# Heads-last pieces in DRAM, eight transfers a stack, and another order at a step's end, in a kernel of four layers

## What is computed

```python
x = x + sliding_window_attention(layernorm(x))   # 32 heads of 8, window 128, blocks of 128 tokens
x = x + ffn(layernorm(x))                        # 256 -> 1024 -> 256, relu, 4-bit weights + rank 16
x = x + delta_layer(layernorm(x))                # see below
x = x + ffn(layernorm(x))                        # same weights as the second
```

```python
h = rms(x); q, k, v = silu(silu(conv4(h @ Wqkv)))    # causal convolution over 4 tokens
q, k = l2norm(q), l2norm(k);  beta = sigmoid(h @ Wbeta)
for each token:  err = S @ k - v;  S = S - beta * outer(err, k);  o = S @ q    # S: 8 x 8 per head
x = x + rms(o) @ Wout;  x = x + (silu(h2 @ Wgate) * (h2 @ Wup)) @ Wdown        # h2 = rms(x)
```

## Time and profile before

| | us |
|---|---|
| median of 3 runs (1444.98 to 1447.88) | 1446.38 |
| the profiled execution | 1451.55 |
| its span in the profile | 1449.8 |
| PE busy | 1098.5 (76%) |
| DVE busy | 938.5 (65%) |
| ACT busy | 509.6 (35%) |
| POOL busy | 174.2 (12%) |

### The profile page before, as it was taken

How to read it: one execution, slowest core, us unless ns; L and a number is a source line. 1 busy time by engine, 2 the same in 40 slices (tenths; PEclk the granted TensorE clock), 3 DMA queues, 4 the chain that set the end, 5 groups by cost and what they waited for, 6 DMA issues and landing times.

```text
span 1449.8 us, 22244 instructions
## 1 busy us (share of the span) xinstructions
PE 1098.5 (76%) x8593; PEld 738.9 (51%) x8600; DVE 938.5 (65%) x2409; ACT 509.6 (35%) x1041; POOL 174.2 (12%) x251
## 2 busy tenths in 40 slices
PE   5478778676778897879779896879778887980587
PEld 3144534453446654656446653656456644750465
DVE  2712368686877577765777577765776688768701
ACT  1033254226323543236323542335322633350121
POOL 2000000301030002100040002100040004011300
PEclk9578879879979998899878998899889998995689
DMA  9524224401530134102520135003410220020000
GB/s 292 75 19 61 22 66 53 39 30 59 61 30 23 30 73 54 9 30 73 59 25 22 36 76 48 7 30 77 63 18 22 67 18 1 15 66 0 14 8 8
DMA packets 112489, 64.57 MB, mean 45 GB/s; under 512 B 49472, under 2 KB 106752, under 8 KB 112384
## 3 DMA queue, kind: packets, MB, share of 16 engines
q1 hardware_dynamic: 106256, 57.61, 23.2%
q10 hardware_dynamic: 6128, 5.54, 1.5%
HBM read 45.55 MB, written 17.17 MB: 43 GB/s over the span
## 4 chain that ended last, share of the span: by engine, by line
PE 49%; DVE 23%; DMA 9%; ACT 8%; SPq 5%; issue 3%; ACTq 2%; POOL 1%; DVEq 0%; POOLq 0%
PE bank L1410 7%; PE bank L1660 6%; PE bank L1402 6%; PE bank L1587 4%; DMA q_stack<-m_rows 4%; PE bank L1679 4%; PE bank L1515 4%; DVE lane_buf L1144 3%; PE bank L1466 3%; DVE state L1163 3%; DVE state L1156 3%; DMA k_stack<-k_pieces 3%; DVE u_l L1151 3%; DVE mx L965 2%; PE bank L1495 2%
## 5 line engine op out<-in xcount | busy, mean ns | idle before, releaser
L680 ACT ACTIVATE probs<-bank 128x512 f32<-128x512 f32 x256 | 151.1, 597 | 276.6 <-PE bank L1500 271.6
L1515 PE MATMUL bank<-probs,v_ext 128*9 128x128 f32 x2048 | 169.8, 288 | 24.9 <-ACT probs L680 23.2
L965 DVE TENSOR_REDUCE mx<-bank 128x2 f32<-128x320 f32 x256 | 120.8, 485 | 103.5 <-PE bank L1466 99.4
L1660 PE MATMUL bank<-feat_c,wgu 128*128 128x256 f32 (+1 forms) x384 | 108.0, 441 | 53.0 <-DVE hid_c L1211 45.7
L1495 PE MATMUL bank<-tri_mask,identb 128*128 128x512 bf16 x256 | 106.9, 417 | 43.6 <-DMA q_stack<-m_rows 43.6
L1461 PE MATMUL bank<-edge_mask,identb 128*128 128x64 bf16 x512 | 64.0, 211 | 91.3 <-DVE mx L965 54.3
L334 POOL TENSOR_TENSOR lane_buf<-state,q_l 128x128 f32<-128x128 f32 x128 | 83.7, 682 | 334.6 <-DVEq L1169 334.6
L1515 PEld LDWEIGHTS bank<-probs,v_ext 128*9 128x9 f32 x2048 | 85.7, 93 | 71.1 <-issue 24.1
L1660 PEld LDWEIGHTS bank<-feat_c,wgu 128*128 128x128 f32 (+1 forms) x384 | 81.0, 216 | 76.8 <-DVE hid_c L1211 47.6
L1144 DVE TENSOR_TENSOR lane_buf<-state,til 128x128 f32<-128x128 f32 x256 | 102.4, 400 | 17.7 <-POOL lane_buf L567 10.1
L1461 PEld LDWEIGHTS bank<-edge_mask,identb 128*128 128x128 bf16 x512 | 33.9, 103 | 145.3 <-DVE mx L965 69.5
(11 more groups left out here) (160 smaller groups left out, 1785.1 us busy)
## 6 DMA issues: line engine op xcount, KB each, us to landing
k_stack<-k_pieces SPq DMA_DIRECT2D x192, 64.0 KB
q_stack<-q_pieces SPq DMA_DIRECT2D x192, 32.0 KB
k_l<-lane_k SPq DMA_DIRECT2D x8, 512.0 KB, 3.7
q_l<-lane_q SPq DMA_DIRECT2D x8, 512.0 KB, 4.7
q_pieces<-conv SPq DMA_DIRECT2D x24, 128.0 KB, 2.1
k_pieces<-conv SPq DMA_DIRECT2D x48, 64.0 KB, 2.0
tok<-in_x SPq DMA_DIRECT2D x8, 256.0 KB, 2.8
x_in<-in_x SPq DMA_DIRECT2D x8, 256.0 KB, 2.8
```

The lines of the kernel that those rows point to most:

```text
L680: act.activation(probs[:, u % 2], score_bank[u % 2][:], ACT.Exp, scale=float(DK) ** -0.5).then_inc(exp_done, 1)
L965: dve.tensor_reduce(mx[:, g, 2 * v:2 * v + 2], bank[1 + u % 2][:, 0:2 * SPAN].rearrange("p (h k) -> p h k", h=2), AX.X, ALU.max).then_inc( ...
L1515: last = pe.matmul(bank[5][row:row + VE, col:col + W], v_ext[:, b, kb, h, :], probs[:, u % 2, (hp * 2 + kb) * W:(hp * 2 + kb + 1) * W], st ...
L1660: last = pe.matmul(late_bank[i % 2][0:m, g * BT:(g + 1) * BT], wgu[:, k, g * INTER + 128 * i:g * INTER + 128 * i + m], fc[:, k], start=(k ...
```

## The change

- **Pieces in DRAM.** q's and k's columns are computed with the head as the last index (two ACT copies at the start permute `wqkv_a`, from a staging area `qk_staged`), so a row of a stack (one of the head's 8 numbers, all 16 heads of a half) is one run in DRAM: 4 KB for q, 8 KB for k, whose two blocks lie side by side and are therefore stored twice (`late`). A load has 8 DMAs in place of 13: zero rows, three of q with 16 rows, two of k with 16 rows, two of k with 8. A store has 9 DMAs as before, all of 256 B runs, but each k piece goes out twice. The pad is stored by 3 DMAs in place of 6.
- **Maxima rows.** One DMA on SP (`load_max`), behind the stack loads in SP's program, in place of three on ACT.
- **Order at a step's end.** `mlp_down` behind the delta projections and output sums; the output product and sums of squares behind it; the last FFN's up product in one piece of 8, its down product in one piece behind `pairs`. `late_tile` keeps the second half of both hidden tiles in a part of `lane_buf`; so POOL's `values_til` waits for the down product.
- **Pairs and substitution** of block n stand at the end of the body in which its projections are, not at the start of the next one, ahead of `result` on DVE. The layer norm of block n+2's input is there too. The scan is taken to begin at u = 5, and `PASS1`, `NEXT_AT` and the other tables are moved.
- `terms_of`: on DVE one instruction of 512 elements for four of 128. On ACT the scaling of y (`y_scale`) comes before the third norm's, inside attention.

```diff
-BEGIN = 8
-PASS1 = {14: (0, 0, 1), 15: (0, 2, 3), 16: (0, 4, 5), 17: (0, 6, 7)}
-PASS1.update({25 + v: (1, v) for v in range(8)})
+BEGIN = 5
+PASS1 = {13: (0, 0, 1), 14: (0, 2, 3), 15: (0, 4, 5), 16: (0, 6, 7)}
+PASS1.update({20 + v: (1, v) for v in range(8)})
-NEXT_AT = {"rstd": 3, "turn": 6, "queries": 8, "keys": 9, "second": 11, "third": 13}
-PAIRS_AT = 4
-TURN_AT = 20
+NEXT_AT = {"turn": 1, "queries": 3, "keys": 4, "second": 6, "third": 8}
+TURN_AT = 19
+TURN_NEXT_AT = 30
...
+Q_PIECES = [(0, 2 * DK, (0, 0)), (2 * DK, 2 * DK, (1, 1)), (4 * DK, 2 * DK, (0, 2))]
+K_PIECES = [(0, 2 * DK, (0, 1)), (2 * DK, 2 * DK, (0, 1)), (4 * DK, DK, (2,)), (5 * DK, DK, (0,))]
-        q_pieces = nc.dram_tensor("q_pieces", (NB, 3, HH, 128, B, W), BF16, kind="Internal").ap()
-        k_pieces = nc.dram_tensor("k_pieces", (3, HH, 128, B, W + T), BF16, kind="Internal").ap()
+        q_pieces = nc.dram_tensor("q_pieces", (NB, 3, HH, B, 128, W), BF16, kind="Internal").ap()
+        k_pieces = nc.dram_tensor("k_pieces", (NB + 1, 3, HH, B, 128, 2, W), BF16, kind="Internal").ap()
...
             def load_stacks(n, g):
...
-                for at, (i, j) in enumerate(PIECE_PAIRS):
-                    rows = slice(at * DK, (at + 1) * DK)
-                    sp.dma_start(q_stack[rows, r], q_pieces[n:n + 1, i, hh, :, b, :].rearrange(
-                        "n (h d) t -> d (n h) t", d=DK)).then_inc(stacks_in[r], 16)
-                    sp.dma_start(k_stack[rows, r], k_pieces[j, hh, :, b, n * W:n * W + 2 * W].rearrange(
-                        "(h d) t -> d h t", d=DK)).then_inc(stacks_in[r], 16)
+                qs = q_pieces[n, :, hh, b].rearrange("p (d h) t -> p d (h t)", d=DK)
+                ks = k_pieces[n, :, hh, b].rearrange("p (d h) k t -> p d (h k t)", d=DK)
+                for into, of, pairs in ((q_stack, qs, Q_PIECES), (k_stack, ks, K_PIECES)):
+                    for row, rows, ps in pairs:
+                        if len(ps) == 1:
+                            src = of[ps[0]]
+                        elif ps[0] == ps[1]:
+                            src = of[ps[0]:ps[0] + 1].broadcast_to([2, DK, of.shape[2]])
+                        else:
+                            src = of[ps[0]:ps[1] + 1:ps[1] - ps[0]]
+                        sp.dma_start(into[row:row + rows, r].rearrange("p h t -> p (h t)"), src
+                                     ).then_inc(stacks_in[r], 16)
...
             def pieces_to_dram(n):
...
-                    for hh in range(HH):
-                        sp.dma_start(k_pieces[p, hh, :, :, n * W + W:n * W + 2 * W],
+                    for late in range(2):
+                        sp.dma_start(k_pieces[n + late, p, :, :, :, 1 - late].rearrange("h b p t -> p (h b) t"),
...
+            def load_max(n, g):
+                sp.wait_ge(m_copied, n * NG + g + 1)
+                sp.dma_start(q_stack[MROW:MROW + 3, slot(n, g)], m_rows[:, g % 2, :]).then_inc(m_in[slot(n, g)], 16)
...
+                if following:
+                    load_max(n, 3)
+                if front:
                     next_stacks(n + 1, 1)
+                    load_max(n + 1, 0)
                     next_stacks(n + 1, 2)
+                    load_max(n + 1, 1)
...
+                if n >= 2:
+                    pool.wait_ge(ffn_c_done, n - 1)
                 pool.tensor_copy(first[:, :, :, :, DK], til[:, :, :, DK:KV].rearrange("p c i v -> p c v i")
...
             def max_rows(n, g):
...
-                for j in range(3):
-                    act.dma_start(q_stack[MROW + j:MROW + j + 1, slot(n, g)], m_rows[j * HPH:(j + 1) * HPH, g % 2, :]
-                                  ).then_inc(m_in[slot(n, g)], 16)
...
+            for k in range(KT):
+                last = act.copy(wqkv_a[:, k, 0:2 * D].rearrange("p (a d h) -> p a d h", d=DK, h=HPH),
+                                qk_staged[:, k].rearrange("p (a h d) -> p a d h", d=DK, h=HPH))
...
             def terms_of(engine, cs, steps=range(C)):
...
-                for v in range(VR):
-                    engine.tensor_tensor(out_terms[:, v, :, i, 0:DK], state[:, cs, v, :, C], qc[:, i, cs, :], ALU.mult)
+                if engine is nc.vector:
+                    engine.tensor_tensor(out_terms[:, :, :, i, 0:DK],
+                                         state[:, cs, :, :, C].rearrange("p c v k -> p v c k"),
+                                         qc[:, i:i + 1, cs, :].broadcast_to([128, VR, n_c, DK]), ALU.mult)
...
+                if following:
+                    til_first(n)
+                if n + 2 < NB:
+                    norm_next_apply(n + 2)
+                if following:
+                    pair_scale(n)
+                    for j in range(C - 1):
+                        til_column(n, j)
                 if tail:
                     result(s)
...
             def body(t, scan=True, tail=True, following=True, front=True):   # TensorE
...
-                if tail:
-                    mlp_down(s)
                 if following:
                     turn_a(n, 3)
-                    beta_in(n, front)
+                    beta_in(n, tail, front)
                     delta_in(n, front)
                     if scan:
                         output_sums(t, front)
                 if tail:
+                    mlp_down(s)
+                if following:
+                    if scan:
+                        output_product(t)
+                    square_sums(n)
+                if tail:
...
                     turn_c(s, 2)
-                    ffn_c_up(s, 0, HALF, following)
...
+                    ffn_c_up(s, 0, FT, following)
+                if following:
+                    pairs(n)
                 if tail:
-                    ffn_c_down(s, 0)
-                    ffn_c_up(s, HALF + 2, FT, following)
-                    ffn_c_down(s, 1)
+                    ffn_c_down(s)
```

More of the change, by code:

```diff
@@ L497, in _ @@
             load_x(1)
+            for g in range(DONE_EARLY):
+                load_max(0, g)
             body(-1, scan=False, tail=False)
@@ L815, in body @@
                 if following:
-                    attention(n, scan, front)
-                elif scan:
-                    pairs_out(t)
+                    attention(n, scan, tail, front)
                 if tail:
-                    y_scale(s)
+                    if not following:
+                        y_scale(s)
+                    turn_c(s, 1)
                 if following:
@@ L1125, in between @@
                     dn, g, step = PIECES_AT[at]
-                    before = max_piece(n + dn, g, step, before)
+                    if front or not dn:
+                        before = max_piece(n + dn, g, step, before)
                 if at in MAX_AT:
@@ L1692, in body @@
                     attention(n, scan, front)
-                elif scan:
-                    pairs(t)
                 if tail:
```

188 lines of the change are left out of this document (87 added, 101 removed).

## The result

The changed kernel takes 1496.6 us (median of 4 runs, 1493.18 to 1498.99) against 1445.74 of the kernel before (4 runs): ratio 1.0331, 95% interval 1.0295 to 1.0366. It is slower by 3.3%. The profiled execution takes 1495.14 us, its span is 1493.3.

A forecast was written before the change was run, and what follows sets the result against it. No engine is full; PE leads, with stack loads' duration on its path. Terms -4.5 - 0.4 - 3.8 - 5.0 - 0.2 - 2 = -15.9 take the profiled 1451.55 to 1435.7, median 1430.5 us; range 1370 to 1462.

The forecast's parts named there:

- rival B: Stack loads stay slow: above 11.3 us a load the saving is used up, at 12.2 us the time is 1458; chance 0.23.
- The length of a load (10.2 us): Stack load, about 12.2 us before: 8 issues take 2.8 us, the 7.4 to 7.6 behind the last stay.
- The rule quoted from the Trainium skill: Engines per transfer: largest number up to 16 dividing both patterns' slowest dimension; two for pair transfers, so 11.8 us a load.
- What a us of load costs (14 us): Each us of stack load adds one to each of two PE waits in each of seven attentions.
- Attention without the load's length: A step's attention: pairs and the 6.6 us maxima wait go, load waits of 3.2 and 4.4 come; -2.0 us.
- The end of a step (+4.2): From F, the MLP's down product before, delta projections after, to V, the next block's first values: 4.2 us longer than 42.45.
- tok_c (-3.2): PE's wait for the turned tok_c: y_scale moves ahead, so 3.2 of 3.6 us a step go.
- The first two blocks (-0.4, -3.8): First block: waits +1.4, ACT's issues -1.8, so -0.4 us; second: attention -2.0, issues -1.8, so -3.8.
- The start (-4.5): Start to the first block's values: no maxima issues on ACT, earlier third load, values at 77 for 81.46 us.
- The tail (-2 for the merged terms): Kernel's end: 16 output-term instructions a block become 4, on the path only where nothing follows; -2 us, bounds 0 and -5.
- Rival A: Stack loads become fast, 6 us or less, both waits gone, -53 us, to about 1377; chance 0.33.

The follow-up runs named there:

- e2: The changed kernel with 12 loads of 8 rows and one of zero rows in place of its 8 transfers a load: 1446.35 us, ratio to before 0.9989.
- e1: The changed kernel with pieces side by side in DRAM and pairs reordered, so each transfer reads contiguous rows: 1357.87 us, ratio to before 0.9381.
- e10: e1 with 16 unused PE products in the wait for feat_c ahead of the last FFN's up product: 1359.76 us, ratio to before 0.9365.
- e4: The kernel before with only the change's DRAM layout and 8 transfers a load, order, tables and maxima as before: 1446.94 us, ratio 0.9994.
- e7: e1 with the output terms on DVE again as four instructions of 128 elements: 1357.88 us, ratio to before 0.9365.

## Why the prediction was wrong

It said 1430.5 and is 66 us off, on the other side of no change. The direction of rival B was right, and its point, 11.3 us a load, was passed: a load takes 13.2. The 66 us divide so: at e2's load of 10.75 my own price gives 1438, 8 us more; e2 took 1446, another 8 for the terms that aren't loads; and from e2 to the changed kernel, which differ in the load's transfers alone, are 50.

- **The length of a load (10.2 us) failed.** The step was: the issues shrink from 13 to 8, "and the 7.4 to 7.6 behind the last stay". Neither held. The 8 issues take 4.4 us and not 2.8, and 8.8 us pass behind the last. What stays behind the last issue isn't a property of the destination alone. With two engines the drain is set by 448 KB at 25 GB/s for each, 9.0 us. The rule quoted from the Trainium skill ("DMA: Bandwidth & Descriptors", how many engines k) described it: this trace shows 0.12, e2 0.56, e1 0.93. By the rule the estimate was 11.8, and I gave it the smaller chance because the row of 8 destination rows looked nearer. e2 shows what my 10.2 stood for, loads with 8 rows: 10.75. The prediction lets the rule agree with the 0.68 of before; by the rule its transfers of 8 rows use 8 engines, a share of 0.50, so that the agreement was loose.
- **What a us of load costs (14 us) was too little.** Between e2 and the changed kernel lie 2.4 us of load (10.75 to 13.2) and 50 us of time, some 20 for each. The waits lie where I put them, and each us counts twice a step; in addition the granted clock is down behind each wait (after the one of 6.94 us the first values take 1.04 us for 0.62), and the start, with three loads in a row, is 6.7 us later than in e2.
- **Attention without the load's length** was right in kind: pairs gone, maxima wait gone, waits of 3.2 and 4.4 forecast and 3.32 and 4.20 in e2. In the changed kernel the part is +1.6 in place of -2.0, with waits of 5.75 and 6.94. The sum had a slip too: V+21.4 and the terms behind it give 67.2 and not 68.0, so -2.9, 4 us in five steps and in the wrong direction.
- **The end of a step (+4.2) was mis-sized**: +7.9. The chain was the right one (F is 1159.53; lanes at F+26.9 in place of 25.3, `til_first` at F+35.6 in place of 34.7), but the columns wait for the pairs, which stand behind an up product of 10.2 us that I reckoned at 7.0, at the clock of before. e10 shows that the idle ahead of it is the cause. One us more was lost before that, with the delta projections at 0.63: the copy to feat_c, forecast at F+27.1, ends at F+28.2. The term is +7.2 in e1 too, so it has nothing to do with loads.
- **tok_c (-3.2)**: the wait fell by 2.9, from 3.6 to 0.7; the stretch it lies in gained only 0.9, as PE's work in it takes 10.0 us and not 8.0, at a granted clock of 0.63.
- **The first two blocks (-0.4, -3.8)** were +15.9 and +5.1. The first is 123.0 in e4, with the same transfers and the old order, and 123.8 in e1, with fast loads and the new order, so order and slow loads do it together. One wait is new, and no term of mine had it: PE stands 8.7 us for the products ahead of the pairs in each of the two blocks without a tail, and the next scores are queued behind. It is there in e1 too.
- **The start (-4.5)** was +4.2: V of block 0 at 85.6, in e1 at 71.8.
- **The tail (-2 for the merged terms)**: last V to the end fell by 8.5, and in e7 no part of it comes from merging. The scan starts right behind V there too; that it ends sooner for it, where nothing else follows, is how I read the gain, and no run tests it. The sign was right, the reason wrong.
- **Rival A** (fast loads: 1377) is what e1 did: 1357.87. The mechanism and even the size were right, and it was one layout away.
